# A vision tower's first layer norm on token rows, with the state-space matrices made between its chunks

## What is computed

```python
def _layernorm(x, axis=-1, eps=1e-05):
    m = jnp.mean(x, axis=axis, keepdims=True)
    v = jnp.var(x, axis=axis, keepdims=True)
    return (x - m) / jnp.sqrt(v + eps)
...
Bu_r = jnp.einsum('blh,ph->blp', x, B_bar_r)      # likewise Bu_i
_, _, xs_r, xs_i = jax.lax.associative_scan(binop, (A_r, A_i, Bu_r, Bu_i), axis=1)
ys = jnp.einsum('blp,hp->blh', xs_r, C_real) - jnp.einsum('blp,hp->blh', xs_i, C_imag)
return jax.nn.gelu(ys + D * x, approximate=False)
```

## Time and profile before

| | us |
|---|---|
| median of 3 runs (lowest, highest) | 690.77 (689.91, 691.05) |
| the profiled execution: its time | 688.56 |
| the profiled execution: its span, first to last instruction | 686.5 |
| mean granted TensorE clock, share of full speed | 0.946 |
| busy in the span: PE, PEld, DVE, ACT, POOL | 608.6, 435.9, 495.9, 263.6, 403.8 |

### The profile page before, as it was taken

One profiled execution on the slowest core, in us unless ns is written; L12 is line 12 of the kernel. 1 busy time (PEld: TensorE's weight loads), 2 busy tenths in 40 slices (PEclk: granted clock), 3 DMA queues, 4 the chain that ended last, 5 costly groups with the idle time before them and its releaser, 6 DMA issues. The chain is left out here.

```text
span 686.5 us, 9721 instructions
## 1 busy us (share of the span) xinstructions
PE 608.6 (89%) x3015; PEld 435.9 (64%) x3015; DVE 495.9 (72%) x948; ACT 263.6 (38%) x689; POOL 403.8 (59%) x562
## 2 busy tenths in 40 slices
PE   0799899967967899999973899999999999999995
PEld 0477777754745787878752466666666666666662
DVE  6688888873895787888832567777777777777664
ACT  2132223224651222222225555555555555545310
POOL 1689999610351133333345167778777777778756
PEclk9999999997977999999985599999999999999998
DMA  6200000000000000000000000000000000000001
GB/s 249 48 1 0 0 1 1 0 0 1 0 0 1 0 1 1 0 0 0 1 0 0 1 1 16 16 17 16 17 16 16 16 16 15 3 16 17 15 17 31
DMA packets 13011, 9.75 MB, mean 14 GB/s; under 512 B 4396, under 2 KB 12716, under 8 KB 12716
## 3 DMA queue, kind: packets, MB, share of 16 engines
q1 hardware_dynamic: 12956, 9.28, 4.4%
q10 hardware_dynamic: 16, 0.00, 0.0%
HBM read 5.08 MB, written 4.20 MB: 14 GB/s over the span
## 5 line engine op out<-in xcount | busy, mean ns | idle before, releaser
L1374 PE MATMUL ex_pE<-ex_WdP,ex_hid 128*128 128x512 f32 x774 | 205.9, 408 | 0.0
L1374 PEld LDWEIGHTS ex_pE<-ex_WdP,ex_hid 128*128 128x128 f32 x774 | 140.0, 189 | 44.3 <-DVE ex_ms L1514 7.7
L1514 DVE TENSOR_TENSOR ex_ms<-ex_pE,ex_gate 128x512 f32<-128x512 f32 x129 | 88.9, 689 | 73.3 <-PE ex_pE L1374 71.4
L1669 POOL TENSOR_TENSOR ex_s<-ex_ms 128x1024 f32<-128x1024 f32 (+1 forms) x33 | 82.4, 2497 | 66.0 <-DVE ex_ms L1514 66.0
L723 DVE TENSOR_TENSOR inv_prod<-inv_pW,m_img 128x504 f32<-128x504 f32 x144 | 91.7, 681 | 17.4 <-PE inv_pW L638 15.7
L1195 POOL TENSOR_TENSOR hT<-hT,ssm_gelu 128x512 f32<-128x512 f32 x32 | 47.7, 1509 | 95.8 <-ACT ssm_gelu L1168 95.8
L649 PE MATMUL inv_pS<-ident,inv_prod 128*128 128x128 f32 x576 | 87.8, 275 | 6.1 <-DVE inv_prod L723 5.4
L649 PEld LDWEIGHTS inv_pS<-ident,inv_prod 128*128 128x128 f32 x576 | 70.0, 141 | 28.6 <-DVE inv_prod L723 20.7
L638 PE MATMUL inv_pW<-inv_ysb,m_conv2L 98*128 98x512 f32 x144 | 69.4, 485 | 2.3 <-DVE inv_ysb L711 2.3
L1438 ACT ACTIVATE ex_hidf<-ex_pH,b1c 128x512 f32<-128x512 f32 (+1 forms) x68 | 45.1, 664 | 60.8 <-PE ex_pH L1327 60.8
L1065 PE MATMUL ssm_y<-ssm_z,N 128*128 128x512 f32 x192 | 52.1, 408 | 6.7 <-DVE ssm_z L1130 6.5
(11 more groups left out here) (238 smaller groups left out, 1022.9 us busy)
## 6 DMA issues: line engine op xcount, KB each, us to landing
m_img<-in_x SPq DMA_DIRECT2D x2, 2048.0 KB, 9.2
out<-ex_res SPq DMA_DIRECT2D x16, 256.0 KB, 2.3
WdT<-in_L_ffn_Wd SPq DMA_DIRECT2D x2, 256.0 KB
W1d<-in_L_ffn_W SPq DMA_DIRECT2D x2, 64.0 KB
bd<-in_L_ffn_bd SPq DMA_DIRECT2D x8, 2.0 KB
m_Bm<-in_L_attn_fwd_B_real SPq DMA_DIRECT2D x2, 16.0 KB, 1.9
m_Bm<-in_L_attn_fwd_B_imag SPq DMA_DIRECT2D x2, 16.0 KB, 2.0
m_Bm<-in_L_attn_bwd_B_real SPq DMA_DIRECT2D x2, 16.0 KB, 2.0
```

The source lines that it names most:

```text
L1374: last = nc.tensor.matmul(pE[n % 3][0:P].rearrange("p e f -> p (e f)"), hid[i % 2][value][:, h, par, 128 * j:128 * j + P], WdP[weight][:, ...
L1514: nc.vector.tensor_tensor(ms[b % NB][0:P, t % TPB, :].rearrange("p (e f) -> p e f", e=EX), pE[n % 3][0:P], gate[i % 2][0:P, t, :].unsqueez ...
L1669: nc.gpsimd.tensor_tensor(s4[0:P, 0:T], m[:, :, 0:4 * F], m[:, :, 4 * F:], ALU.add).then_inc(halved, 1)
```

## The change

The blocks matrices and layer_norm go, and one block norm_and_matrices takes their place. In it a chunk is turned to token rows by the matmul that also takes off the mean (the chunk as weights, center as the moving side), so that the 64 features of a token lie along the columns. ScalarE squares, VectorE sums over the features (total_up), GpSimd makes the variance, ScalarE the root, VectorE the reciprocal (invert), GpSimd the Newton step (refine), VectorE the product (scale), TensorE turns the chunk back (turn_out), ScalarE rounds the high part. The low part is made by VectorE for even chunks, and for odd ones by GpSimd from a second copy. The class tokens are a 17th chunk of 4 rows. Each engine has its list written out turn by turn (k from 0 to 18) with chunks k, k-1 and k-2 in work, and the steps of the matrices block are put at the ends of certain turns. The matrices' tiles live on into the scan, which uses two of them, m.N and m.M, as room for z and act_y. The memsets of KI move from setup into the new block.

```diff
@@ -115,15 +116,15 @@
     with ExitStack() as ctx:
         g = Tower(nc, ctx, arrays, out)
         with ExitStack() as states:
-            g.add_states(nc, states)
-            with ExitStack() as making:
-                m = Matrices(nc, making)
+            g.add_scan(nc, states)
+            m = Matrices(nc, states)
+            with ExitStack() as pictures:
+                m.add_pictures(nc, pictures)
                 setup(nc, g, m)
                 involution(nc, g, m)
-                matrices(nc, g, m)
             g.add_norm(nc, states)
-            layer_norm(nc, g)
-            state_space(nc, g)
+            norm_and_matrices(nc, g, m)
+            state_space(nc, g, m)
         experts(nc, g)
...
-                fill(g.mean2[:], 0.0)
-                fill(g.mean2[0:64, 0:1], 1.0 / F)
-                fill(g.mean2[64:128, 1:2], 1.0 / F)
...
-                for n in range(2):
-                    nc.gpsimd.memset(g.KI[n][:].bitcast(F32), 0.0)
...
-def matrices(nc, g, m):
...
-def layer_norm(nc, g):
...
+def norm_and_matrices(nc, g, m):
+    ITEMS = NCH + 1
+    TPI = 2 * TILES
+    NC, NU = 3, 2
...
         with nc.Block() as block:
             @block.tensor
             def _(pe):
+                def turn_in(i):
+                    if i >= NC:
+                        pe.wait_ge(normed, i - NC + 1)
+                    for j in range(columns(i)):
+                        src = g.hC[:] if is_cls(i) else hflat[:, i * CH + 128 * j:i * CH + 128 * j + 128]
+                        last = nc.tensor.matmul(pC[i % NC][0:rows(i), 128 * j:128 * j + 128], src, g.center[:],
+                                                start=True, stop=True)
+                    last.then_inc(centered, 1)
+                def turn_out(i):
+                    pe.wait_ge(normed, i + 1)
...
+                    P = rows(i)
+                    for j in range(columns(i)):
+                        last = nc.tensor.transpose(pU[i % NU][:, 128 * j:128 * j + P],
+                                                   xn[i % 2][0:P, 2 * j:2 * j + 2, :].rearrange("p r f -> p (r f)"), g.ident[0:P, 0:P])
+                    last.then_inc(turned, 1)
...
+                for k in range(ITEMS + 2):
+                    if there(k):
+                        turn_in(k)
+                    if there(k - 2):
+                        turn_out(k - 2)
+                    if k == 1:
+                        for d in range(2):
+                            first = 0 if d == FWD else 1
+                            ins = nc.tensor.matmul(pK[:, d, :, :], m.M0[:, d, :, :], m.N[:, 0, d, first:first + 4, :],
+                                                   start=(d == 0), stop=(d == 1), skip_group_check=True)
+                        ins.then_inc(k_made, 1)
+                    if k == 3:
+                        weights(0, 8)
+                    if k == 12:
+                        weights(8, len(LV_PLAN))
             @block.scalar
             def _(act):
...
+                    nc.scalar.activation(sq[i % 2][0:P, 0:T, :].rearrange("p t f -> p (t f)"), pC[i % NC][0:P, 0:F * T],
+                                         ACT.Square).then_inc(squared, 1)
...
+                    nc.scalar.activation(root[i % 2][0:P, 0:T], var[i % 2][0:P, 0:T], ACT.Sqrt).then_inc(rooted, 1)
                 def high(i):
+                    act.wait_ge(turned, i + 1)
+                    if is_cls(i):
+                        nc.scalar.copy(g.uC[:], pU[i % NU][:, 0:B]).then_inc(high_made, 1)
+                        return
+                    if by_pool(i):
...
+                        nc.scalar.copy(whole[i // 2 % 2][:], pU[i % NU][:])
+                    nc.scalar.copy(uflat[0][:, span(i)], pU[i % NU][:]).then_inc(high_made, 1)
+                for k in range(ITEMS + 2):
+                    if there(k - 1):
+                        take_root(k - 1)
+                    if there(k):
+                        squares(k)
+                    if there(k - 2):
+                        high(k - 2)
+                    if k == 4:
+                        nc.scalar.copy(g.N[0][:], m.N[:]).then_inc(highs, 1)
+                    if k in (6, 8, 14):
+                        n = (6, 8, 14).index(k)
+                        c = 4 if n < 2 else 3
+                        act.wait_ge(m_turned, n + 1)
+                        nc.scalar.copy(g.LV[0][:, 4 * n:4 * n + c, :], pT[n % 2][:, 0:c, :]).then_inc(highs, 1)
             @block.vector
             def _(v):
...
+                    nc.vector.tensor_tensor(xn[i % 2][0:P, 0:T, :], pC[i % NC][0:P, 0:F * T].rearrange("p (t f) -> p t f", f=F),
+                                            factor[i % 2][0:P, 0:T].unsqueeze(2).broadcast_to([P, T, F]), ALU.mult).then_inc(normed, 1)
...
+                    nc.vector.reciprocal(guess[i % 2][0:P, 0:T], root[i % 2][0:P, 0:T]).then_inc(guessed, 1)
...
+                    nc.vector.tensor_reduce(total[i % 2][0:P, 0:T], sq[i % 2][0:P, 0:T, :], AX.X, ALU.add).then_inc(summed, 1)
...
+                def low(i):
+                    v.wait_ge(high_made, i + 1)
+                    nc.vector.tensor_tensor(uflat[1][:, span(i)], pU[i % NU][:], uflat[0][:, span(i)], ALU.subtract).then_inc(low_made, 1)
...
+                def inputs_high(d):
...
+                    for r in (lo, hi):
+                        last = nc.vector.scalar_tensor_tensor(out=K0[r, d, :], in0=g.ident[r, r], scalar=m.raw[r, 3, d:d + 1],
+                                                              in1=power(d, 0)[r], op0=ALU.mult, op1=ALU.add)
+                    last.then_inc(step, 1)
+                    v.wait_ge(step, 2 * d + 1)
+                    for r, which, j, k in plans[d]:
+                        last = nc.vector.tensor_copy(g.KI[0][r, d, which, j, :], value(d, r, k))
+                    last.then_inc(step, 1)
+                def inputs_low(d):
...
+                    for r, which, j, k in plans[d]:
+                        nc.vector.tensor_tensor(g.KI[1][r, d, which, j, :], value(d, r, k), g.KI[0][r, d, which, j, :],
+                                                ALU.subtract)
+                def weights_low(n):
...
+                    nc.vector.tensor_tensor(g.LV[1][:, 4 * n:4 * n + c, :], pT[n % 2][:, 0:c, :], g.LV[0][:, 4 * n:4 * n + c, :],
+                                            ALU.subtract).then_inc(lv_parted, 1)
+                for k in range(ITEMS + 2):
+                    if there(k - 2):
+                        scale(k - 2)
+                    if there(k - 1):
+                        invert(k - 1)
+                    if there(k):
+                        total_up(k)
+                    if there(k - 2) and not by_pool(k - 2) and not is_cls(k - 2):
+                        low(k - 2)
+                    if k in (5, 9):
+                        inputs_high((k - 5) // 4)
+                    if k in (7, 11):
+                        inputs_low((k - 7) // 4)
+                    if k in (8, 10, 16):
+                        weights_low((8, 10, 16).index(k))
             @block.gpsimd
             def _(pool):
...
+                    nc.gpsimd.tensor_scalar(var[i % 2][0:P, 0:T], total[i % 2][0:P, 0:T], 1.0 / F, LN_EPS, ALU.mult, ALU.add).then_inc(varied, 1)
...
+                    pool.wait_ge(guessed, i + 1)
+                    nc.gpsimd.tensor_tensor(c, y, y, ALU.mult).then_inc(newton, 1)
+                    pool.wait_ge(newton, 3 * i + 1)
+                    nc.gpsimd.tensor_tensor(c, c, x, ALU.mult).then_inc(newton, 1)
+                    pool.wait_ge(newton, 3 * i + 2)
+                    nc.gpsimd.tensor_scalar(c, c, -0.5, 1.5, ALU.mult, ALU.add).then_inc(newton, 1)
+                    pool.wait_ge(newton, 3 * i + 3)
+                    if i >= 2:
+                        pool.wait_ge(normed, i - 1)
+                    nc.gpsimd.tensor_tensor(o, y, c, ALU.mult).then_inc(factored, 1)
...
+                def low(i):
+                    pool.wait_ge(high_made, i + 1)
+                    nc.gpsimd.tensor_tensor(uflat[1][:, span(i)], whole[i // 2 % 2][:], uflat[0][:, span(i)],
+                                            ALU.subtract).then_inc(low_by_pool, 1)
+                nc.gpsimd.tensor_copy(g.hC[0:F, 1:B], g.hC[0:F, 0:1].broadcast_to([F, B - 1])).then_inc(emptied, 1)
+                pool.wait_ge(emptied, 1)
+                for n in range(2):
+                    last = nc.gpsimd.memset(g.KI[n][:].bitcast(F32), 0.0)
+                last.then_inc(emptied, 1)
+                for k in range(ITEMS + 2):
+                    if there(k - 1):
+                        variance(k - 1)
+                        refine(k - 1)
+                    if there(k - 2) and by_pool(k - 2):
+                        low(k - 2)
+                    if k == 7:
+                        pool.wait_ge(highs, 1)
+                        nc.gpsimd.tensor_tensor(g.N[1][:], m.N[:], g.N[0][:], ALU.subtract)
...
-        z = [sb(f"z{n}", [128, CH]) for n in range(2)]
```

(86 more changed lines are left out.)

256 lines of the change are left out of this document (68 added, 188 removed).

## The result

The changed kernel takes 681.14 us (median of 4 runs, 680.96 to 685.89). Its ratio to the kernel before is 0.9883, with a 95% interval of 0.9843 to 0.9923. That is faster by about 8 us, and outside the range of the prediction: 688.8 was forecast, with 686.2 as the lower end. Executions of the kernel before at 695 us and more (7 of 73) are of a second, slower kind and are left out of every mean.

The account below looks back on a forecast made before the run. No engine was taken to fill the 63.7 us stretch; a round trip over four engines would pace the new block. 60.6 us gains 3.1, less 1.1 for half clock: 690.77 - 2.0 = 688.8 us, range 686.2 to 693.0.

Parts of the forecast that it names:

- The path: New block: a round trip over four engines, with variance behind GpSimd's low part, sets the pace at 3.1 us a chunk.
- First scale: Start of the new block: turn_in, Square, table load, root, invert, refine and hand-overs sum to 4.9 us.
- a clean pair: New block: two chunks, from one odd scale to the next, take 6.2 us; seven pairs make 43.4.
- the subtraction for N: GpSimd, turn 7 of the new block: stands in front of variance, on the path, and costs 2.9 us.
- the clock: TensorE in the new block: half clock lengthens turn_out in odd turns, 0 to 3.9 us, taken as 1.1.
- a cover for the matrices: New block: the norm by itself wins next to nothing; the matrix steps, 11.7 us before, cost 6.0 between the chunks.
- weights_low: VectorE, even turns of the new block: stands between low and the next scale and costs 1.7 us.
- The cast that reads K0: VectorE, turns 5 and 9: held by GpSimd's low it costs 1.4 us a turn, free 0; 1.4 taken in all.
- The whole of what can be won or lost: The 63.7 us of matrices block and first norm; involution, scan and experts keep their instructions.
- the prediction's own sign: Whole kernel: the prediction fails if anything outside the new block moves.
- Half clock all through: Rival, new block: TensorE at half clock throughout, 64.5 us, so +0.8 and 691.6 us; chance 0.22.
- The matrices were not paid in full: Rival, new block: inserted matrix steps go unhidden, 14.2 us in place of 6.0, so 697.0 us; chance 0.14.

Follow-up runs that it names:

- the experts' start kept busy: 63 matmuls with unread results added at the start of the experts' block: 678.81 us on the changed kernel, 687.39 on the kernel before.
- the kernel with them apart: Changed kernel with the matrix steps taken out of the turns into a block of their own ahead of the new norm: 694.83 us, ratio 1.0055.
- the thirteen: Executions of the unaltered changed kernel: the first four and nine of a repeat run (median 684.67 us); mean of all 683.1 us.
- the kernel fed with 38 matmuls: Kernel before with 38 matmuls, results unread, added behind TensorE's part of the matrices block: 685.75 us, ratio 0.9956.

## Why the prediction was wrong

**The path and most prices were right.** First scale at 4.70 us (4.9 predicted), first odd scale at 7.36 (7.5), a clean pair 6.1 (6.2), the subtraction for N 2.89 (2.9), the block 59.94 and 60.95 us, and 60.34 with the experts' start kept busy (61.7 with the clock). That what is won is a cover for the matrices is borne out by the kernel with them apart. The terms that were off: weights_low cost 1.2 in place of 1.7, as the third one lies in the last pair (6.10 us), where the class chunk's short sum (0.27) leaves room for it, and from the last odd scale to the next block it is 4.64 us, where 3.9 - 0.5 + 0.3 = 3.7 had been put. GpSimd's load of a pair, put at 4.2 us, is 3.9 by the prices given; nothing rests on it.

**The cast that reads K0** had been given 1.4 us, half of two holds. It was not held in the first profile; in the second it was held by 1.04 us, in turn 5 alone, and that pair took 7.47 us in place of 6.75. With the experts' start kept busy it was held there too, and the pair took 7.32. The cast of the first profile, then GpSimd's subtraction and the cast of the second:

```profile
163.98 0.19 DVE L859 CAST KI<-nm_K 64x64 fp32r<-64x64 f32 x1
```

```profile
163.79 1.26 POOL L916 TENSOR_TENSOR u<-nm_whole,u 128x512 fp32r<-128x512 f32 x1 [0.66 <-ACT u L798]
...
163.88 1.23 DVE L859 CAST KI<-nm_K 64x64 fp32r<-64x64 f32 x1
```

In the first, the cast began 0.17 us before the subtraction (164.15) and took 0.19 us; in the second 0.09 us after it began, and it ended with it. The Trainium skill says the same of the two engines (SBUF — State Buffer, Who interferes with whom): where VectorE works in a mode that uses both of its ports, as a cast can, whichever was issued first holds the shared pair for its whole instruction. The clock had a part in it: in the first profile it fell to half at 162.3 us, the odd chunk was turned out in 0.91 us in place of 0.66, and the subtraction began 2.83 us behind its scale in place of 2.58.

**The step that failed is the clock.** The prediction took the old stretch as 63.7 us, and the old norm as 3.2 us a chunk, from one execution whose clock was 0.80 and 0.83 there, and charged half clock to the new block alone: -1.1 of a gain of 3.1. That the old stretch has two times, by its clock, was put at nothing.

In the new block the charge of 1.1 us was large enough. The pair of turn 9 took 7.15, 7.13 and 7.14 us in the three profiles, 0.45 over 6.10 and the 0.60 of weights_low, and the odd chunk's turn_out shows why. In the clean pair and in turn 9:

```profile
191.70 0.66 PE L743 MATMUL nm_pU<-ident,nm_xn 128*128 128x128 f32 x4 [1.60 <-DVE nm_xn L822]
```

```profile
178.47 1.12 PE L743 MATMUL nm_pU<-ident,nm_xn 128*128 128x128 f32 x4 [5.05 <-DVE nm_xn L822]
```

The pair of turn 5 took 6.75 us at half clock, 0.65 over a clean one with the inserted casts in it, but 7.32 at full clock with the cast held: there the half clock cost less than the hold that it spared. So the block does not follow its clock: 59.94, 60.95 and 60.34 us at 0.82, 0.85 and 0.90.

The old stretch does. Its two chunks take 1.85 us longer at half clock; its 63.7 us was that of an execution in which the clock was high in the norm's loop, and 70.47, at 0.73, that of another. Three profiles of the old stretch (63.69, 70.47, and 63.60 with the experts' start kept busy) average 65.9 us, three of the new one 60.4: a gain of 5.5, of the 6.3 us between the means of the times. For single executions it goes from 2.7 (63.60 - 60.95) to 10.5 (70.47 - 59.94). Against the 2.0 us forecast, the old stretch is 2.2 us longer than the prediction took it, the new one 1.3 shorter, and 0.8 lie outside the stretch or in the choice of executions; three profiles a side are few for such a mean. The first four executions gave about 8 us, 1.8 more than the thirteen, which is luck.

What takes the cost away is that TensorE does not pace the new block. In the first pair of profiles the mean clock of the stretch is 0.82 before and after, so by estimate some 22 us were at half clock in both. That the idle matrices block sets off the half clock in the old norm is argued and not shown: the kernel fed with 38 matmuls is 3 to 4 us faster on the mean, yet the clock fell in the norm of its profiled execution.

**"The whole of what can be won or lost" was wrong as well.** Scan and experts keep their instructions, but not their time: the experts took 327.60 and 323.56 us in two executions of the same kernel, by the clock of their first 36 us (0.53 and 0.72). In the first pair of profiles scan and experts added 3.9 us to the gain, of which none is the change's as far as the experiments show: with TensorE kept busy there, both kernels have the same experts' block. By the prediction's own sign, that something outside the block moves, it had failed.

**The rivals.** Half clock all through did not come, with 0.82 and 0.85 in the block. The page TensorE: Matmul & The Clock Gate of the Trainium skill (Part 4: PE-mode transpose) would have put it on the transposes. But the clock also fell at 165.3 us of the kernel fed with 38, behind 5.3 us in which TensorE was busy 4.98 with matmuls alone. The matrices were not paid in full: of 14.2 us unhidden, 4.1 were on the path of the first profile (5.2 with the clock and the casts of turn 5). None of the rivals had the old kernel's clock as its subject, and so the range ended at 686.2.

What stays open is what decides in which execution the clock falls where; the runs show how often the times differ, not why.

## What to carry to other kernels

Before a sum is made against a stage's time, read at which clock that stage ran, and what one turn of its loop takes at either level: a stage that TensorE paces at half clock has two times, and a change that hands the pace to another engine takes that difference away. Whether this alone wins is not shown here: the new norm by itself, 56.7 us, was no faster than the old one, and the gain lay in the cover for the matrices. A path walked in the written order gave a pair of turns to 0.1 us; the work that is inserted between turns is hidden only as far as the slack of the shorter turn goes, so price it again when the turn gets shorter.

## What the runs showed of the hardware

The clock fell to half behind a stretch in which the profile calls TensorE 94% busy (4.98 of 5.3 us), and stayed at 0.50 through stretches in which it was busy all the time (10.2 of 10.2 us, 3.00 of 3.00). Four transposes took 0.66 us at full clock and 1.12 at half. Some 0.3 us in the start of a cast from SBUF decide whether it takes 0.19 us or 1.23 beside a GpSimd subtraction, while a product with one operand in PSUM took 0.69 beside one.
